# A vision-transformer layer with expert routing: the GELU outputs transposed for the row store on VectorE in 32x32 blocks, and the image loop written out

## The reference

```python
h = patches @ Wp + bp + pos                       # 8 x 1024 tokens x 256
h = h + attn(layernorm(h))                        # 8 heads of 32, sigmoid gate
x = layernorm(h)                                  # input of the feed-forward part
H = gelu(x @ W1 + b1)                             # 8192 tokens x 1024 features
probs = softmax(H @ Wg + bg); assign = argmax(probs)
for e in range(8):
    y = H @ Wd[e] + bd[e]
    out = out + where(assign == e, probs[:, e:e+1] * y, 0)
h = h + out
```

## Time and profile before

| | us |
|---|---|
| three runs | 1952.97, 1954.45, 1948.21 (median 1952.97) |
| the profiled execution, its own time | 1954.93 |
| its span on the core | 1952.8 |
| busy TensorE (matmul) / VectorE / ScalarE / GpSimd | 1728.6 / 1151.3 / 1012.5 / 309.7 |
| stage 1 ends (last logits kept) | 1574.6 |
| stage 2 ends (sort done, first gather) | 1659.8 |

### The profile page before, as it was taken

How to read it: one execution, slowest core, us unless ns; L and a number is a source line. 1 busy time by engine, 2 the same in 40 slices (tenths; PEclk the granted TensorE clock), 3 DMA queues, 4 the chain that set the end, 5 groups by cost and what they waited for, 6 DMA issues and landing times.

```text
span 1952.8 us, 32763 instructions
## 1 busy us (share of the span) xinstructions
PE 1728.6 (89%) x11396; PEld 1180.4 (60%) x11396; DVE 1151.3 (59%) x1899; ACT 1012.5 (52%) x1692; POOL 309.7 (16%) x239
## 2 busy tenths in 40 slices
PE   8587899999998999999899999999797724899998
PEld 4354456646655574566467555745363614899998
DVE  0347767467655856675667468566726278344443
ACT  1144756675574657566746656585666350222222
POOL 0200100200010020002000200200000061455554
PEclk9898999999999999999999999999899867899999
DMA  3133042313413140424033222413040160566663
GB/s 112 34 98 98 1 103 77 125 30 99 112 65 82 63 133 28 103 69 133 18 103 92 93 65 73 129 39 87 17 135 1 60 220 1 200 205 199 208 204 132
DMA packets 68112, 187.59 MB, mean 96 GB/s; under 512 B 14173, under 2 KB 14829, under 8 KB 67824
## 3 DMA queue, kind: packets, MB, share of 16 engines
q1 hardware_dynamic: 51952, 121.48, 22.0%
q0 software_dynamic: 16000, 63.98, 10.0%
HBM read 84.72 MB, written 51.38 MB: 70 GB/s over the span
## 4 chain that ended last, share of the span: by engine, by line
PE 72%; DVE 14%; issue 8%; ACT 4%; DMA 1%; SPq 1%; POOL 0%; DVEq 0%; ACTq 0%; POOLq 0%
PE ps L477 12%; PE ps L738 11%; PE ps L491 10%; PE ps L444 8%; DVE nmax L1029 6%; PE ps L548 3%; PE ps L465 3%; PE ps L726 3%; PE ps L549 3%; PE ps L550 3%; PE ps L527 3%; PE ps L505 3%; PE ps L576 3%; ACT pr L842 2%; DVE oh L1084 2%
## 5 line engine op out<-in xcount | busy, mean ns | idle before, releaser
L1029 DVE TENSOR_REDUCE nmax<-ps 128x1 f32<-128x1024 f32 x512 | 625.2, 1222 | 315.1 <-PE ps L477 305.5
L842 ACT ACTIVATE pr<-ps,nmax 128x1024 f32<-128x1024 f32 x512 | 569.9, 1113 | 295.8 <-DVE nmax L1029 290.6
L477 PE MATMUL ps<-stk,stq 96*128 96x512 f32 x1024 | 407.3, 480 | 80.2 <-ACT pr L842 54.1
L477 PEld LDWEIGHTS ps<-stk,stq 96*128 96x128 f32 x1024 | 168.5, 193 | 282.7 <-ACT pr L842 169.0
L491 PE MATMUL ps<-pr,vs 128*32 128x256 f32 x4096 | 275.9, 391 | 16.7 <-DVE vs L948 16.6
L738 PE MATMUL ps<-wd,hg 128*128 x1728 | 225.5, 287 | 0.0
L339 POOL TENSOR_SCALAR vare<-mv 128x8 f32<-128x8 f32 x24 | 5.7, 238 | 1349.8 <-DVE mv L903 1349.8
L738 PEld LDWEIGHTS ps<-wd,hg 128*128 128x128 f32 x1728 | 212.7, 192 | 0.0
L491 PEld LDWEIGHTS ps<-pr,vs 128*32 128x32 f32 x4096 | 109.8, 110 | 166.6 <-issue 75.5
L879 ACT ACTIVATE hg<-ps 128x512 fp32r<-128x512 f32 x144 | 78.5, 596 | 249.6 <-PE ps L726 249.6
L444 PE MATMUL ps<-wp,xt 128*128 128x256 f32 x768 | 198.3, 385 | 1.6 <-DMA xt<-x_in 0.8
(11 more groups left out here) (123 smaller groups left out, 1944.2 us busy)
## 6 DMA issues: line engine op xcount, KB each, us to landing
token_rows<-staged SPq DMA_DIRECT2D x128, 256.0 KB, 2.0
xt<-x_in SPq DMA_DIRECT2D x64, 384.0 KB, 3.1
stq<-qk SPq DMA_DIRECT2D x192, 128.0 KB, 2.4
stk<-qk SPq DMA_DIRECT2D x192, 128.0 KB, 2.5
token_rows<-hres POOLq DMA_DIRECT2D x8, 1024.0 KB, 5.2
wd_raw<-w_down SPq DMA_DIRECT2D x16, 512.0 KB, 4.0
rows<-token_rows,slot_from POOLq DMA_INDIRECT x72, 4.7
out<-rows,slot_to POOLq DMA_INDIRECT x72, 2.6
```

Source lines behind the costliest of these rows:

```text
L477: last = mm(ps[:, 2 * (k % SR) + j, :], stq[:, hh, i * P:(i + 1) * P], stk[:, hh, j * 512:(j + 1) * 512], start=True, stop=True)
L842: actv(pr[:, k % PR, :], ps[:, 2 * (k % SR):2 * (k % SR) + 2, :].rearrange("p a n -> p (a n)"), ACT.Exp, bias=nmax[:, k % 16:k % 16 + 1], ...
L1029: V.reduce_max(nmax[:, k % 16:k % 16 + 1], ps[:, 2 * (k % SR):2 * (k % SR) + 2, :].rearrange("p a n -> p (a n)"), AX_X, negate=True).then_ ...
```

## The change

- The transposes of `ht` on TensorE (`turn_hidden`), the copies on ScalarE (`stage_hidden`) and their waits (`hu_mm`, `hu_read`) are gone.
- VectorE transposes each chunk `ht[:, k, :]` in 32x32 blocks straight from SBUF to SBUF (`block_turn`): of block j of 32 tokens and block i of 32 features, partition 32i+r gets token 32j+r. There are two staging buffers (kg = 0 and 1), each holding four chunks of 512 tokens, 8 KB a partition. `staged_b` (kg = 0) lies in the memory that attention steps from 34 on write again, so the exponential of step 34 waits for its stores (`row_out[0]`).
- A store is now four DMAs, one for each 32 partitions, each 32 x 16 pieces of 128 floats (512 B) where it was 128 rows of 512 floats (2 KB). A row of 512 features stands in the order (i, k, c) and not (k, i, c), and the experts' weights are loaded to match: each piece by four DMAs of 32 partitions with runs of 256 floats.
- All stores of an image come behind `load_stack(b, 1)` on SyncE.
- `ht` of the second half may be written once VectorE has transposed the first half's chunk (`hu_done`). `lt` moves into `xt`.
- Images are written out one by one on every engine; the loop of stage 1 is gone.

```diff
+block_view = token_rows.rearrange("(b h j r) d -> b h r j d", b=IMAGES, h=2, r=BLK)
...
         def over_images(eng, body):
-            body(0, 0, False, True)
-            with eng.Fori(0, (IMAGES - 2) // 2) as j:
-                body(j * 2 + 1, 1, True, True)
-                body(j * 2 + 2, 0, True, True)
-            body(IMAGES - 1, (IMAGES - 1) % 2, True, False)
+            for b in range(IMAGES):
+                body(b, b % 2, b > 0, b < IMAGES - 1)
...
             def store_hidden(b, u):
-                hf, kg, t = u // 8, u // 4 % 2, u % 4
-                hold(sp, "hu_read", b * 16 + u + 1)
-                sp.dma_start(rows_view[b, :, 4 * hf + t, kg * HALF:(kg + 1) * HALF], staged[:, u % STAGED, :]
-                             ).then_inc(row_out[u % STAGED], 16)
+                hf, kg = u // 2, u % 2
+                hold(sp, "hu_done", b * 16 + 4 * u + 4)
+                for i in range(P // BLK):
+                    at_col = kg * HALF + i * P
+                    sp.dma_start(block_view[b, hf, :, :, at_col:at_col + P],
+                                 staged[kg][i * BLK:(i + 1) * BLK].rearrange("r j k c -> r j (k c)")
+                                 ).then_inc(row_out[kg], 16)
...
-                    sp.dma_start(wd_raw[:, i], w_down[j * WD_BUFFERS + i]).then_inc(wd_in[i], 16)
+                    piece = w_down[j * WD_BUFFERS + i].rearrange("(i n) k d -> k n i d", n=BLK)
+                    for k in range(P // BLK):
+                        sp.dma_start(wd_raw[k * BLK:(k + 1) * BLK, i], piece[k]).then_inc(wd_in[i], 16)
...
-                    if k >= 4:
-                        turn_hidden(b, k - 4)
...
                         wait(act, "ff_mm", b * 16 + 8 * hf + k + 1)
                         if hf == 1:
                             wait(act, "lg_mm", b * 2 + 1)
-                            wait(act, "hu_mm", b * 16 + 4 * (k // 4) + 4)
+                        wait(act, "hu_done", b * 16 + 8 * hf + k - 7)
                         actv(ht[:, k, :], spare(bank), ACT.Gelu, bias=bf1[:, k:k + 1]).then_inc(S["ff_act"], 1)
-                        if hf == 1 or k >= 4:
-                            stage_hidden(b, 8 * hf + k - 4)
...
+                    if before and k == G_STEPS + 2:
+                        wait(act, row_out[0], b * 8 * 16)
...
+            def block_turn(b, hf, k):
+                kg = k // 4
+                wait(dve, "ff_act", b * 16 + 8 * hf + k + 1)
+                if k % 4 == 0:
+                    wait(dve, row_out[kg], (b * 2 + hf) * 4 * 16)
+                V.transpose(staged[kg][:, :, k % 4, :], ht[:, k, :].rearrange("p (j r) -> p j r", r=BLK)
+                            ).then_inc(S["hu_done"], 1)
```

More of the change, by code:

```diff
@@ L44 @@
 RING = 6
-STAGED = 4
+STAGED = 2
+BLK = 32
+CB = HALF // BLK
 WD_BUFFERS = 4
@@ L118, in vit_layer_kernel @@
         gate = tensor(sa, "gate", [P, DC, TOKENS])
-        staged = tensor(sa, "staged", [P, STAGED, HALF])
+        staged_a = tensor(sa, "staged_a", [P, CB, 4, BLK])
         turned = ExitStack()
@@ L294, in image @@
             def image(b, par, before, after):
-                load_stack(b, 0, False)
+                load_stack(b, 0)
                 if after:
@@ L300, in image @@
                     load_rest(b + 1)
-                load_stack(b, 1, before)
+                load_stack(b, 1)
                 if before:
-                    for u in range(4, 16):
+                    for u in range(4):
                         store_hidden(b - 1, u)
             over_images(sp, image)
-            for u in range(16):
+            for u in range(4):
                 store_hidden(IMAGES - 1, u)
@@ L567, in turn_logits @@
                 last.then_inc(S["lg2_mm"], 1)
-            def turn_hidden(b, u):
-                hf, kg, t = u // 8, u // 4 % 2, u % 4
-                wait(pe, "ff_act", b * 16 + 8 * hf + 4 * kg + 4)
-                if u >= 4:
-                    wait(pe, "hu_read", b * 16 + u - 3)
-                for q in range(4):
-                    last = nc.tensor.transpose(ps[:, u % 4, q * P:(q + 1) * P],
-                                               ht[:, 4 * kg + q, t * P:(t + 1) * P], ident[:])
-                last.then_inc(S["hu_mm"], 1)
             def router(b):
@@ L599, in router @@
                     hidden(b, 1, k, 1 if k == 1 else k)
-                    turn_hidden(b, 4 + k)
-                for u in range(12, 16):
-                    turn_hidden(b, u)
             def front_start(b):
@@ L647, in image @@
                             router(b - 1)
-                    if before and k in (G_STEPS, G_STEPS + 1):
-                        wait(pe, "hu_read", b * 16 + 2 * (k - G_STEPS) - 2)
                     score(b, k)
@@ L852, in image @@
                         high(b + 1, 0, QK0_AT[k][0])
-                if before:
-                    for i in range(STAGED):
-                        wait(act, row_out[i], b * (16 * 16 // STAGED))
             over_images(act, image)
@@ L1020, in image @@
                             norm_1(b + 1, 1 - par)
+                        if before:
+                            for c in range(4):
+                                block_turn(b - 1, 0, c)
+                        if after:
                             stats_2(b + 1)
                         if before:
+                            for c in range(4, HC):
+                                block_turn(b - 1, 0, c)
                             logit_sums(b - 1, 0)
@@ L1027, in image @@
                         gated(b, 0)
+                        if before:
+                            for c in range(HC):
+                                block_turn(b - 1, 1, c)
                     wait(dve, "score_mm", b * STEPS + k + 1)
@@ L1056, in _ @@
             for hf in range(2):
+                for c in range(HC):
+                    block_turn(last_b, hf, c)
                 logit_sums(last_b, hf)
```

28 lines of the change are left out of this document (10 added, 18 removed).

## The result

The changed kernel takes 1892.18 us (median of four runs, 1889.04 to 1894.45); the kernel before, beside it on the same chip, 1953.31. The ratio is 0.969 (95% interval 0.967 to 0.971). The profiled execution spans 1889.2 where before spanned 1952.8, so 63.6 went. One execution of the kernel before, 3330 where all others took 1948 to 1958, was disturbed and is left out everywhere.

A forecast was written before the change was run, and what follows sets the result against it. TensorE was taken to set the pace, with room on VectorE. Gains of 30 (router stretch), 4.2 (last image), 7.6 (loop) and 3 (expert weights) sum to 44.8, say 44, off 1954.93: 1911 us, range 1896 to 1935.

The forecast's parts named there:

- part 1: Router stretch, images 1 to 7: transposes moved from TensorE to VectorE gain 4.3 an image, 30 in seven.
- part 3: Stage 1 loop: two jumps back removed, saving issue gaps and one slow first group; 7.6, up to 10.3.
- wait for the last store: End of stage 1: the last store lands after the logits need it, giving back 2.1.
- part 2: Last image: path to the last logits 6.3 earlier, less 2.1 for the last store; gain 4.2.
- part 4: Expert weights: four loads a piece start GpSimd after L1084, so VectorE is not shut out there; 3, between 0 and 9.
- the failed step of part 1: Router stretch: table load, exponential and step 34 keep their distances behind step 32's maximum; exponential at 32.5.
- The new wait of TensorE: Router stretch, after the next hidden chunk: TensorE waits about 2.0 for VectorE's copy of the first half's logits.
- rival 5: Stage 1 loop: taking the jumps away gives nothing, jumps being cheap or stalls appearing elsewhere; 1918, chance 0.09.
- Rival 1: Router stretch: half-rate block transposes (time T) bound VectorE, step 32's maximum at 17.9 + 16T; 1964, chance 0.06.
- Rival 2: Stores: the number of pieces sets their price, 90 ns each, delaying step 34's exponential; 2010, chance 0.03.
- Rival 3: Router stretch, second half: GpSimd's addition of `hres` shuts out the block transposes; 1952, chance 0.06.
- Rival 4: Router stretch: TensorE's clock falls in its new wait, 2.8 more in each of seven images; 1930, chance 0.06.

The follow-up runs named there:

- table_late: Changed kernel with ScalarE's two waits ahead of step 32's exponential swapped in images 1 to 6, so the table load waits for the maximum; 1901.74 us.
- turned_only: Changed kernel with the kernel before's stage 1 loop, one load DMA per weight piece and, for the first half, no ScalarE wait on `hu_done`; 1929.56 us.
- loop_back: Changed kernel with images 3 to 6 run by a loop of two turns again, the other images written out; 1905.23 us.
- turned_copy_first: turned_only with the logits' copy ahead of the first half's last four block transposes on VectorE; 1908.67 us.
- two_loads: Changed kernel with each expert weight piece loaded by two DMAs of 64 partitions where it has four; 1890.92 us.
- one_load: Changed kernel with each expert weight piece loaded by one DMA of 128 partitions with 4 KB runs; 1898.92 us.

## Why the prediction missed

The forecast added up to 44.8, the traces differ by 63.6:

| | said | in the traces |
|---|---|---|
| images 1 to 6 without the jumps and the clock of the loop (part 1) | 25.8 | 29.6 |
| the loop (part 3) | 7.6 | 14.0 |
| image 7 to the last logits (parts 1 and 2) | 4.3 + 6.3 | 15.3 |
| wait for the last store (part 2) | -2.1 | -3.6 |
| sort (part 4) | 3 | 8.0 |
| the rest | 0 | 0.3 |

The direction and the engine that sets the pace were right. No single term explains the miss; the loop and the sort are the largest. With the failed step of part 1 alone put right, 8 of it, the forecast would have been about 1903, still inside the range.

**Part 1, the router stretch (30).** Sizes inside it were right: GELU pitch 1.40, transposes 0.62, the wait for the logits' copy there, the last transpose 0.7 behind the last GELU, the maximum at 29.1 where 29.9 was said (30.6 in images 2, 4 and 6). The new wait of TensorE was 0.95 and not 2.0, since VectorE came to the copy at 16.0 and not 16.8. The step that failed is the sentence "What stands behind the maximum (table load, exponential, step 34) keeps its distances." The table load moved ahead of the maximum: the exponential came at 30.3, 32.5 was said. The rows of before already held the hint: the load at 375.34 waits for `nmax`. Image 7 of before, without that wait, showed that the place is not fixed. I read it as fixed; it was the loop's register waits, and the change takes the loop away. It is worth 1.4 an image up to the exponential, 8 in six; table_late, which puts the load back behind the maximum, lost 9.6. The exponential came 5.8 earlier on the mean of images 1 to 6, 34.7, where 4.3 x 6 = 25.8 was said. Against it, 0.7 of it in images 1, 3 and 5 and 1.0 in the others is gone again within the image; in image 1 the clock is at 0.66 from 371 to 376, at 1.00 at that place in before. That leaves 29.6. Image 7 is not like the six: VectorE has no norms in it, TensorE does not wait for the copy, and the exponential came 6.8 earlier.

**Part 2, the last image (4.2).** The last router stretch gained 8.0 (39.25 to 31.23), not 6.3; in before it ran in part at the lower clock. From the start of image 7 to the last logits the kernels with block transposes take 219.0 to 228.5, by how long the clock is at half there, so the 15.3 of the table carries some 5 of that either way. The wait for the last store is 3.7 and not 2.1, because issue took 0.3 to 1.5 a DMA (median 1.0 from `staged_a`) where 0.33 to 0.59 was assumed, and landing 4.5. Net 4.4: two errors that cancel.

**Part 3, the loop (7.6, up to 10.3).** The chain of before holds 2.69 + 2.05 of issue and 2.82 + 2.73 of slow first groups, 10.3, and about 1.2 more in each of images 3 to 5 from the clock in their steps: some 14. (What the changed kernel loses in its longer images 2, 4 and 6, 1.8 each, is already taken off in part 1.) I counted what stands *at* the jump; what a loop does to the waits *inside* the body I left out. With it, writing the images out is worth 18 in the kernel before and 31 with the block transposes.

The Trainium skill (Advanced Engine Details and Errata, Control Flow Timing) has 51 and 108 ns for a branch. The jumps of turned_only, loop_back and turned_copy_first show 2.1 to 3.5 of issue each; here the trace decides, and rival 5 is out.

**Part 4, the expert weights (3, between 0 and 9).** The gain is 8.0 in the traces, and 6.7 and 7.3 by experiment: inside its bounds by luck, for another reason. I argued that L1084 would start ahead of GpSimd. It starts 0.15 behind it, as before. What changed is that the loads come at 224 to 233 GB/s and no longer in a burst at up to 420, so GpSimd works off no stock, and VectorE's operations slip in one at a time: 2.27 each, even for eight elements.

**The rivals.** Rival 1's formula held to 0.1 where its T was made real. Rival 2 is out: stores were waited for 1.2 in all within the images. Rival 3 is out: the transposes kept 0.67 to 0.71 beside GpSimd's addition of `hres`. Rival 4 did happen, in three of six images, at 1.55 each and not 2.8; I gave it 0.06 as a thing of all images or none. Nothing in my list stood on the fast side. The range's low end came from uncertain sizes of known steps alone, though each of the three parts of the change had been costed as if the others were not there.

## What to carry to other kernels

When a change turns register waits into constant ones, or the other way round, look at every table load behind them: a load that stands behind a wait in the trace may be there by that wait alone, and in this kernel the order of two waits in front of one activation moved an exponential by 1.34 in each of six images, and the median by 9.6. Cost parts of a change in the state that the other parts leave behind, and ask of each what it would run into by itself. Where VectorE fills TensorE's gaps, put the one operation that TensorE waits for ahead of the bulk: here one moved line gave 10.0 in six images, and more than half of that was not the wait itself but the clock that fell behind it.

## What was not expected of the hardware

- The same 512 KB from the same memory moves at 406 to 420 GB/s in one DMA of 128 partitions and at 234 to 244 in two of 64, with the DMA engines' share at 1.0 in both. The Trainium skill (SBUF — State Buffer, section on the DMA port swizzle) accounts for it, as said under two_loads. Four DMAs of 32 go as slowly; no other set of partitions was tried here.
- The slower loads made the kernel faster by 7, since they starve the engine that shuts VectorE out.
- While GpSimd subtracted, a 128x512 reduction on VectorE took 0.67 and a copy from PSUM 0.69, but scans, an addition, a cast and an int32 shift of 128x8 waited for it, though the last two read one SBUF tile each. The Trainium skill (SBUF — State Buffer, the two separate sides) names such operations: those in a two-port mode, or with two SBUF inputs; the rows agree. It has the lock held for one whole instruction. With gaps between GpSimd's subtractions a VectorE operation waited for one of them, 2.27; without a gap it waited for all sixteen, 37.25. The block transposes were not slowed beside GpSimd's addition.
- TensorE idle for 0.78 and then for 0.95 is followed by a fall of the granted clock in images 2, 4 and 6 of the changed kernel and not in 1, 3 and 5; in one_load the odd images are the longer ones, in table_late the first two. What picks them stays open.
